# Cross-attentions of a decoder on one core: probabilities turned in 32x32 blocks by VectorE and carried by DMAs, the division moved behind the weighted sum

## The chip, the core and the metric

The kernel runs on one core of a Trainium2 chip. The metric is the device time of one execution in microseconds, as a median over runs. All data is fp32. The profile shows TensorE's matmuls (PE) and weight loads (PEld), VectorE (DVE), ScalarE (ACT), GpSimd (POOL), and the queues in which SP and ACT issue DMAs (SPq, ACTq).

## What is computed

Four decoder layers, each with self-attention, cross-attention and a mixture of experts, on x of 8 x 56 tokens of 256 features, each step with a residual and a layer norm. The cross-attentions of layers 0, 2 and 3 are latent attentions over a context of 1500 positions with 64 features. Cut to what matters:

```python
q_r = einsum('bshq,hqr->bhsr', q_big, W_qr)        # after two projections (and rope)
k_r = einsum('bld,hdr->bhlr', kv_r, W_kr)
scores = einsum('bhsr,bhlr->bhsl', q_r, k_r)       # 16 heads, s = 56, l = 1500
attn = softmax(scores, axis=-1)
ctx_c = einsum('bhsl,bld->bhsd', attn, kv_r)
ctx = einsum('bhsd,hkd->bhsk', ctx_c, w_kc_kv) ... @ Wo.T
```

## The kernel before

The twelve steps run one after the other, each as a stage in which every engine has its own program, written out in order; semaphores tie them together. `cross_attention` is the stage of layers 0, 2 and 3. Its first part folds the weights and makes the queries `q2` (16 heads of 56 tokens of 8 samples) and the matrices `cm`. Its second part, which the change is about, works through NU = 28 units. The 8 samples lie in J = 4 pairs, and a pair has UNITS = 7 units of 128 rows (head, token). A unit does the same 128 rows for both samples e = 0 and 1 of the pair, against 1500 positions of each, in LT = 12 blocks of LP = 125. With two samples there are 24 blocks of probabilities in a unit. The context of a sample is 64 features wide, so two matmuls on 64 rows or 64 columns of the array (halves r) go side by side. In the fourth unit of a pair (`SPLIT`) each half is divided between the two samples, so that it takes four matmuls where the others take two.

What a unit i goes through:

- PE, `score(i, k)` (L1035): for k = 0 to 2, 500 positions of each sample, into banks 0 to 2 (e = 0) and 3 to 5 (e = 1). These banks exist once: score(i, 0) waits for both exponentials of unit i - 1.
- DVE, `rowmax(i)`: three reductions of 500 (L1315), one of the three maxima (L1317), and one of 1500 for the other sample (L1320).
- ACT, `exp(i, e)` (L1236): 1500 elements from PSUM to `probs`, with the sum over the row by an accumulator read.
- DVE, `invert` (L1324) and `divide` (L1328): the reciprocal of the sum, and the division of 1500 probabilities, for each e.
- PE, `turn(i, k)` (L1122): 48 transposes (24 blocks of 125, by 64 rows each) into six banks; they leave PSUM in six copies of 512, two by DVE (L1334) and four by ACT (L1243), into `pT`.
- PE, `weigh(i)` (L1135): for each of 12 blocks and each half, `ctx_pos` times `pT`, summed in bank 6, 128 columns.
- DVE, `keep(i)` (L1341): the sum into `held`; POOL (L908) places it in `ctxT`. After the last unit DVE does both (`keep_last`, L1348).

PE's order is score(i), weigh(i - 2), turn(i - 1) for each i, and at the end project(0), weigh(26), project(1), turn(27), project(2), weigh(27), norms, project(3) (`project` is L1150). Each matmul counts as two instructions in the trace, a transpose as one. DVE's order in an iteration is rowmax(i), invert and divide (i, 0), keep(i - 2), its two copies of unit i - 1, invert and divide (i, 1). ACT's is exp(i, 0), exp(i, 1), its four copies of unit i - 1; in iteration 0 it also copies `cm` and the last queries (`cm_out(3)`, `place(7)`, L1195). SP issues the loads of the next stage's weights (`prefetch`, all through L125) once the last queries are placed, about when unit 0 is done.

## Time and profile before

| | us |
|---|---|
| median of 3 runs | 1667.23 |
| lowest, highest | 1664.79, 1677.47 |
| span of the profiled execution, first to last instruction | 1666.3 |
| PE busy (share of the span) | 1627.4 (98%) |
| DVE busy | 1113.9 (67%) |
| ACT busy | 749.9 (45%) |
| POOL busy | 239.1 (14%) |
| stretches of the 28 units of layers 0, 2, 3 (scores to the end of the stage) | 205 to 447, 829 to 1070, 1338 to 1582 |

The profile is of one execution, whose span is the time to which sums are compared; the median of the runs is 0.9 us above it. A group of instructions is named by its line in the kernel, the engine, the operation and the tiles written and read, with count, busy time and mean duration, and behind the last bar the idle time of the engine just before them and what ended it. Durations of neighbours on one engine overlap a little, so a period is read from starts. Matmul ends are modelled.

### The profile page before, as it was taken

Reading aid. Unit: us, or ns where it says so; the run is one execution under the profiler, and the core shown is the slowest. Engines: PE = TensorE matmul, PEld = TensorE weight load, DVE = VectorE, ACT = ScalarE, POOL = GpSimd, SP = SyncE. Lnnn points to the kernel's source line nnn. Section 1 sums busy time; section 2 is a strip of 40 time slices with the busy share of each in tenths; the row PEclk is TensorE's granted clock in tenths of the full one; section 3 lists DMA queues with packets and bytes.
Section 4 is the critical chain, followed back from the end, with each engine's and each line's share of the span. In section 5 each row is a group of like instructions: output and inputs, shape, how many; then the busy total and the mean of one; then the engine's idle time right before and its main releaser. Section 6 shows DMA issues by size and latency. Waiting matters only on the chain.

```text
span 1666.3 us, 35653 instructions
## 1 busy us (share of the span) xinstructions
PE 1627.4 (98%) x15234; PEld 1104.8 (66%) x15234; DVE 1113.9 (67%) x1974; ACT 749.9 (45%) x1297; POOL 239.1 (14%) x428
## 2 busy tenths in 40 slices
PE   9999999999999899999999999999999999999998
PEld 5575367777755666655377777764566767777765
DVE  3735899999566763266899999435445289999623
ACT  2223366666413641144366666312444366666411
POOL 0011300000010313011200000010455000000030
PEclk9999999999999999999999999999999999999999
DMA  8302020000040011051020000050300220000010
GB/s 280 86 13 83 1 78 2 2 2 2 2 187 1 2 59 40 1 133 48 1 97 2 2 2 2 4 240 0 64 1 1 114 89 2 2 2 2 2 44 11
DMA packets 35522, 71.10 MB, mean 43 GB/s; under 512 B 25359, under 2 KB 29775, under 8 KB 31433
## 3 DMA queue, kind: packets, MB, share of 16 engines
q1 hardware_dynamic: 35240, 68.71, 12.6%
q8 instruction: 121, 1.98, 0.5%
q14 instruction: 35, 0.29, 0.1%
q10 hardware_dynamic: 126, 0.11, 0.0%
HBM read 68.36 MB, written 0.46 MB: 41 GB/s over the span
## 4 chain that ended last, share of the span: by engine, by line
PE 89%; DVE 6%; ACT 2%; POOL 1%; issue 1%; DMA 1%; SPq 0%; DVEq 0%; POOLq 0%; ACTq 0%
PE ps L1122 14%; PE ps L1135 14%; PE ps L1035 13%; PE ps L1501 9%; PE ps L361 9%; PE ps L946 3%; PE ps L2599 3%; PE ps L1150 3%; PE ps L528 2%; PE ps L1961 2%; PE ps L956 1%; POOL arena L1795 1%; PE ps L2626 1%; PE ps L982 1%; PE ps L967 1%
## 5 line engine op out<-in xcount | busy, mean ns | idle before, releaser
L1236 ACT ACTIVATE arena<-ps,softmax_stats 128x1500 f32<-128x1500 f32 x168 | 253.8, 1511 | 193.0 <-DVE softmax_stats L1317 190.8
L1135 PEld LDWEIGHTS ps<-arena,ctx_pos 125*64 125x64 f32 x4608 | 222.3, 137 | 58.4 <-issue 55.4
L1122 PE MATMUL ps<-ident,arena 64*125 64x64 f32 x4032 | 239.1, 271 | 1.9 <-ACT arena L1236 1.6
L1135 PE MATMUL ps<-arena,ctx_pos 125*64 125x128 f32 (+1 forms) x4608 | 240.5, 262 | 0.0
L1122 PEld LDWEIGHTS ps<-ident,arena 64*125 64x125 f32 x4032 | 226.8, 185 | 17.0 <-issue 13.5
L1035 PE MATMUL ps<-ctx_feat,arena 64*128 64x500 f32 x1008 | 230.5, 590 | 0.0
L1243 ACT COPY arena<-ps 125x512 f32<-125x512 f32 x336 | 172.5, 600 | 77.9 <-PE ps L1122 77.9
L1315 DVE TENSOR_REDUCE softmax_stats<-ps 128x1 f32<-128x500 f32 x252 | 170.6, 678 | 49.0 <-PE ps L1035 48.6
L361 PE MATMUL ps<-arena 128*128 128x256 f32 x736 | 174.7, 383 | 3.5 <-DVE arena L1630 1.2
L1328 DVE TENSOR_SCALAR arena<-arena,softmax_stats 128x1500 f32<-128x1500 f32 x168 | 168.3, 1002 | 5.9
L1501 PE MATMUL ps<-x_feat,arena 128*128 128x448 f32 (+1 forms) x416 | 167.9, 549 | 1.2 <-DVE arena L1613 1.2
L361 PEld LDWEIGHTS ps<-arena 128*128 128x128 f32 x736 | 137.0, 190 | 40.9 <-issue 16.6
L908 POOL COPY arena<-arena 64x128 f32<-64x128 f32 (+1 forms) x186 | 51.1, 275 | 682.6 <-DVE arena L1341 676.5
L1320 DVE TENSOR_REDUCE softmax_stats<-ps 128x1 f32<-128x1500 f32 x84 | 143.6, 1709 | 0.0
L1035 PEld LDWEIGHTS ps<-ctx_feat,arena 64*128 64x128 f32 x1008 | 89.2, 187 | 80.0 <-issue 77.1
L1501 PEld LDWEIGHTS ps<-x_feat,arena 128*128 128x128 f32 (+1 forms) x416 | 79.3, 193 | 65.7 <-issue 61.7
L1334 DVE COPY arena<-ps 125x512 f32<-125x512 f32 x168 | 107.6, 682 | 12.8 <-PE ps L1122 12.5
L1577 ACT ACTIVATE arena<-ps 128x448 f32<-128x448 f32 (+1 forms) x52 | 28.2, 543 | 187.0 <-PE ps L1501 187.0
L1613 DVE TENSOR_TENSOR arena<-ps,arena 128x448 f32<-128x448 f32 x41 | 25.6, 624 | 115.6 <-ACT arena L1577 87.9
L946 PE MATMUL ps<-x_feat,arena 128*128 128x448 f32 x128 | 56.1, 563 | 0.2
L2599 PE MATMUL ps<-x_feat,arena 128*128 128x448 f32 x128 | 52.4, 552 | 1.2 <-issue 0.7
L2727 DVE TENSOR_TENSOR arena<-ps,arena 128x448 f32<-128x448 f32 x32 | 20.0, 625 | 46.0 <-ACT arena L2671 45.9
(324 smaller groups left out, 1931.7 us busy)
## 6 DMA issues: line engine op xcount, KB each, us to landing
ctx_pos<-in_ctx SPq DMA_DIRECT2D x1, 2688.0 KB
arena<-in_L1f_gate SPq DMA_DIRECT2D x1, 2304.0 KB, 12.1
arena<-in_L1f_up SPq DMA_DIRECT2D x1, 2304.0 KB, 17.0
arena<-in_L1f_down SPq DMA_DIRECT2D x1, 2304.0 KB, 7.8
arena<-in_L0a_Wq SPq DMA_DIRECT2D x1, 2048.0 KB, 10.9
arena<-in_L0a_Wc SPq DMA_DIRECT2D x1, 2048.0 KB, 18.8
arena<-in_L0x_Wq SPq DMA_DIRECT2D x1, 2048.0 KB, 9.9
arena<-in_L0x_Wo SPq DMA_DIRECT2D x1, 2048.0 KB, 8.3
```

The costliest lines, as they stand in the source:

```text
L361: m = c.nc.tensor.matmul(y_of(c, s, j), lhsT, rhs, start=False, stop=last, skip_group_check=True)
L946: m = nc.tensor.matmul(c.ps[:, 2 + h % 2, 0:NT], wq[:, k, h, :], c.x_feat[:, k, :, 0:T], start=(k == 0), stop=(k == KT - 1))
L1035: m = nc.tensor.matmul(sc[e][:, k, :], q[e * 64:(e + 1) * 64], c.ctx_feat[e * 64:(e + 1) * 64, j, k * 4 * LP:(k + 1) * 4 * LP], start=True ...
L1122: m = nc.tensor.transpose(c.ps[0:LP, turn_bank(i, k, r), n * 64:(n + 1) * 64], probs[i % 2][e][rows, l * LP:(l + 1) * LP], c.ident[rows, r ...
L1135: m = nc.tensor.matmul(y[r * 64:(r + 1) * 64, lo:hi], c.ctx_pos[:, j, l, e, :], pT[i % 2][:, lo // 64:hi // 64, LT * e + l, :], start=(l = ...
L1236: nc.scalar.activation(probs[i % 2][e].rearrange("p (k l) -> p k l", k=3), sc[e], ACT.Exp, bias=low[:, i % 4, e:e + 1], accum_out=total[:, ...
L1243: nc.scalar.copy(pT[i % 2][:, r, 8 * k:8 * k + 8, :], c.ps[0:LP, turn_bank(i, k, r), :].rearrange("p (s q) -> p s q", s=8)).then_inc(*a_in ...
L1315: nc.vector.tensor_reduce(peak[:, i % 4, k:k + 1], sc[0][:, k, :], AX.X, ALU.max).then_inc(*maxed.next())
L1320: nc.vector.tensor_reduce(low[:, i % 4, 1:2], sc[1], AX.XY, ALU.max, negate=True).then_inc(*lowered[1].next())
L1328: nc.vector.tensor_scalar(probs[i % 2][e], probs[i % 2][e], inv[:, i % 4, e:e + 1], None, ALU.mult).then_inc(*normed[e].next())
L1334: nc.vector.tensor_copy(pT[i % 2][:, r, 0:8, :], c.ps[0:LP, turn_bank(i, 0, r), :].rearrange("p (s q) -> p s q", s=8)).then_inc(*d_in.next())
L1501: m = nc.tensor.matmul(c.ps[0:m_, bank(n) + i, 0:NT], w[:, k, n * 128:n * 128 + m_], c.x_feat[:, k, :, 0:T], start=(k == 0), stop=(k == KT ...
```

## The change

It touches `cross_attention` alone. The exponential writes each block of 125 probabilities with a pitch of LQ = 128. Of the 24 blocks, the first BY_PE = 6 of sample 1 are still turned by PE: 12 transposes in place of 48, into the rest of bank 6 and into bank 7, and they leave PSUM in two copies of 384 by ACT. The other 18 are turned by two VectorE transposes (`turn_blocks`), of 12 x 128 = 1536 and 6 x 128 = 768 elements a partition. Each works in squares of 32x32: position 4q + g of a block goes, for g = 0 to 3, to partition q of a group of 32 in `blocks`, so the transposes read `probs` with a step of four elements. Every square is then on the partitions of its 32 rows, and SP moves it with four DMAs a unit: DMA `frm` reads 32 partitions (rows 32 frm and on), 4 x 576 elements of each, and writes 128 partitions, 576 elements (2304 bytes) of each, into `moved_to`: 288 KB a DMA, 1152 KB a unit. `weigh` takes its moving operand from `moved_to` or from `pT`.

The probabilities are no longer divided. DVE makes both reciprocals of a unit in one instruction after the transposes. POOL multiplies the identity by them (`diag`, two products of 128x128), PE multiplies ones by `diag` (`spread`, two matmuls, four in a split unit), which gives each column its reciprocal on all rows, ACT copies that to `rinv`, and POOL multiplies the held context by it where it copied before. Keeping the sum of `weigh` moves from DVE to ACT. In ACT's order the copies of unit i - 2 and the keeping of unit i - 3 stand ahead of exp(i, 0). The prefetch of the next stage is issued by ACT in iteration 0, as SP's queue holds the moves. Both `blocks` and `moved_to` have two buffers: the transposes of unit i wait until the moves of unit i - 2 have landed, and its moves until weigh(i - 2) is done. PE's order is score(i), weigh(i - 2), turn(i - 1), spread(i - 1).

```diff
-        "C": 23616, "Z": 25664, "buf": 27712, "rope": 3584, "PT": 0, "P": 6144, "RB": 12288}
...
+        "C": 23616, "Z": 25664, "buf": 27712, "rope": 3584, "PT": 0, "P": 6144, "TT": (12288, 25664), "RB": 14592}
...
+LQ, BY_PE = 32 * 4, 6
+RUN = 32 * (2 * LT - BY_PE)
...
-    pT = [c.at(o["PT"] + i * LT * 256, LT * 256, LP).rearrange("p (r s q) -> p r s q", r=2, q=64) for i in range(2)]
-    probs = [[c.at(o["P"] + (2 * i + e) * L, L) for e in range(2)] for i in range(2)]
-    held = [c.at(o["RB"] + 128 * i, 128) for i in range(2)]
...
+    blocks = [c.at(o["TT"][i], 4 * RUN).rearrange("p (g n) -> p g n", g=4) for i in range(2)]
+    moved_to = [c.at(o["PT"] + i * 4 * RUN, 4 * RUN).rearrange("p (g n) -> p g n", g=4) for i in range(2)]
+    pT = [c.at(o["PT"] + 8 * RUN + i * 128 * BY_PE, 128 * BY_PE, LP).rearrange("p (r l q) -> p r l q", r=2, q=64) for i in range(2)]
+    probs = [[c.at(o["P"] + (2 * i + e) * LT * LQ, LT * LQ) for e in range(2)] for i in range(2)]
+    held, rinv = ([c.at(o["RB"] + 256 * n + 128 * i, 128) for i in range(2)] for n in range(2))
+    diag = [c.at(o["RB"] + 512 + 256 * i, 256).rearrange("p (e n) -> p e n", e=2) for i in range(2)]
+    ones = c.at(o["RB"] + 1024, 64)
     low, total, inv = (c.sb_small[:, 8 * n:8 * n + 8].rearrange("p (i e) -> p i e", e=2) for n in range(3))
...
+    def turn_place(r):
+
+        return c.ps[0:LP, 7, 0:64 * BY_PE] if r else c.ps[0:LP, 6, 128:128 + 64 * BY_PE]
+
+    spread_ps = c.ps[:, 7, 64 * BY_PE:64 * BY_PE + 128]
...
-        sp.wait_ge(lat_in.handle, lat_in.at(4 * NH // 2))
-        prefetch(sp)
+        for i in range(NU):
+            sp.wait_ge(blocked[1].handle, blocked[1].at(i + 1))
+            if i >= 2:
+                sp.wait_ge(pv_mm.handle, pv_mm.at(i - 1))
+            for frm in range(4):
+                sp.dma_start(moved_to[i % 2][:, frm, :],
+                             blocks[i % 2][32 * frm:32 * frm + 32, :, :]).then_inc(moved[i % 2].handle, 16)
+                moved[i % 2].n += 16
...
-        for i in range(NU - 1):
+
+        def spread_out(i):
+            pool.wait_ge(recip.handle, recip.at(i + 1))
+            if i >= 4:
+                pool.wait_ge(ct_in.handle, ct_in.last())
+            if i >= 2:
+                pool.wait_ge(spread_mm.handle, spread_mm.at(i - 1))
+            for e in range(2):
+                nc.gpsimd.tensor_scalar(diag[i % 2][:, e, :], c.ident[:], inv[:, i % 4, e:e + 1], 1.0, ALU.mult, ALU.mult).then_inc(*diag_in.next())
+
+        def place_context(i):
             j, u = i // UNITS, i % UNITS
+            pool.wait_ge(diag_in.handle, diag_in.last())
+            pool.wait_ge(rinv_in.handle, rinv_in.at(i + 1))
             pool.wait_ge(kept.handle, kept.at(i + 1))
             for r, e, lo, hi in parts(u):
                 rows, at = slice(r * 64, (r + 1) * 64), 128 * u - HALF * (r ^ e)
-                nc.gpsimd.tensor_copy(ctxT[rows, 2 * j + e, at + lo:at + hi], held[i % 2][rows, lo:hi]).then_inc(*ct_in.next())
+                nc.gpsimd.tensor_tensor(ctxT[rows, 2 * j + e, at + lo:at + hi], held[i % 2][rows, lo:hi],
+                                        rinv[i % 2][rows, lo:hi], ALU.mult).then_inc(*ct_in.next())
+
+        for i in range(NU):
+            spread_out(i)
+            if i >= 3:
+                place_context(i - 3)
+        place_context(NU - 3)
+        place_context(NU - 2)
         pool.wait_ge(ct_in.handle, ct_in.last())
...
-            if i > 1 and k < 2:
-                pe.wait_ge(d_in.handle, d_in.at(2 * (i - 2) + 1 + k))
-            if i > 1 and k == 2:
-                pe.wait_ge(a_in.handle, a_in.at(4 * (i - 2) + 3))
...
-        def turn(i, k):
-
-            if k == turn_order(i)[0]:
-                for e in range(2):
-                    pe.wait_ge(normed[e].handle, normed[e].at(i + 1))
-            if k == 0 and i < NU - 1:
-                pe.wait_ge(exped[0].handle, exped[0].at(i + 2))
-            if k == 2 and i > 0:
-                pe.wait_ge(kept.handle, kept.at(i))
-            if i == 0 and k == 2:
+        def turn(i):
+
+            pe.wait_ge(exped[1].handle, exped[1].at(i + 1))
+            if i == 0:
                 pe.wait_ge(lat_in.handle, lat_in.at(4 * NH // 2))
                 pe.wait_ge(cm_act.handle, cm_act.at(3))
-            if k == (1 if i == 0 else 2) and i < NU - 1:
-                pe.wait_ge(exped[1].handle, exped[1].at(i + 2))
-            for n in range(8):
-                e, l = divmod(8 * k + n, LT)
+            else:
+                pe.wait_ge(b_in.handle, b_in.at(2 * i))
+                pe.wait_ge(rinv_in.handle, rinv_in.at(i))
+            for l in range(BY_PE):
                 for r in range(2):
                     rows = slice(r * 64, (r + 1) * 64)
-                    m = nc.tensor.transpose(c.ps[0:LP, turn_bank(i, k, r), n * 64:(n + 1) * 64],
-                                            probs[i % 2][e][rows, l * LP:(l + 1) * LP], c.ident[rows, rows])
-                    if n == 7:
+                    m = nc.tensor.transpose(turn_place(r)[:, l * 64:(l + 1) * 64],
+                                            probs[i % 2][1][rows, l * LQ:l * LQ + LP], c.ident[rows, rows])
+                    if l == BY_PE - 1:
                         m.then_inc(*(turned_hi if r else turned_lo).next())
 
+        def spread(i):
+
+            pe.wait_ge(diag_in.handle, diag_in.at(2 * i + 2))
+            for r, e, lo, hi in parts(i % UNITS):
+                m = nc.tensor.matmul(spread_ps[r * 64:(r + 1) * 64, lo:hi], ones, diag[i % 2][:, e, lo:hi], start=True, stop=True,
+                                     skip_group_check=True)
+            m.then_inc(*spread_mm.next())
+
         def weigh(i):
 
             j, u = i // UNITS, i % UNITS
-            pe.wait_ge(a_in.handle, a_in.at(4 * (i + 1)))
-            pe.wait_ge(d_in.handle, d_in.at(2 * (i + 1)))
+            pe.wait_ge(b_in.handle, b_in.at(2 * (i + 1)))
+            pe.wait_ge(moved[i % 2].handle, moved[i % 2].at(64 * (i // 2 + 1)))
+            if i > 0:
+                pe.wait_ge(kept.handle, kept.at(i))
             y = c.ps[:, 6, :]
             for l in range(LT):
                 for r, e, lo, hi in parts(u):
-                    m = nc.tensor.matmul(y[r * 64:(r + 1) * 64, lo:hi], c.ctx_pos[:, j, l, e, :],
-                                         pT[i % 2][:, lo // 64:hi // 64, LT * e + l, :], start=(l == 0 and lo == 0),
+                    if e == 1 and l < BY_PE:
+                        p = pT[i % 2][:, lo // 64:hi // 64, l, :]
+                    else:
+                        at = 32 * (LT * e + l - BY_PE * e)
+                        p = moved_to[i % 2][0:LP, lo // 32:hi // 32, at:at + 32]
+                    m = nc.tensor.matmul(y[r * 64:(r + 1) * 64, lo:hi], c.ctx_pos[:, j, l, e, :], p, start=(l == 0 and lo == 0),
                                          stop=(l == LT - 1), skip_group_check=True)
             m.then_inc(*pv_mm.next())
...
-            for k in turn_order(i - 1):
-                turn(i - 1, k)
-        pe.wait_ge(d_in.handle, d_in.at(2 * (NU - 1)))
+            turn(i - 1)
+            spread(i - 1)
         project(0)
         weigh(NU - 2)
         project(1)
-        for k in range(3):
-            turn(NU - 1, k)
+        turn(NU - 1)
+        spread(NU - 1)
...
-            nc.scalar.activation(probs[i % 2][e].rearrange("p (k l) -> p k l", k=3), sc[e],
-                                 ACT.Exp, bias=low[:, i % 4, e:e + 1],
+            nc.scalar.activation(probs[i % 2][e].rearrange("p (k l q) -> p k l q", k=3, l=4)[:, :, :, 0:LP],
+                                 sc[e].rearrange("p k (l q) -> p k l q", l=4), ACT.Exp, bias=low[:, i % 4, e:e + 1],
                                  accum_out=total[:, i % 4, e:e + 1]).then_inc(*exped[e].next())
 
-        def copy_turned(i, k, r):
-            done = turned_hi if r else turned_lo
-            act.wait_ge(done.handle, done.at(3 * i + turn_order(i).index(k) + 1))
-            nc.scalar.copy(pT[i % 2][:, r, 8 * k:8 * k + 8, :],
-                           c.ps[0:LP, turn_bank(i, k, r), :].rearrange("p (s q) -> p s q", s=8)).then_inc(*a_in.next())
-
-        for i in range(NU + 1):
+        def copy_turned(i, r):
+            if r:
+                act.wait_ge(turned_hi.handle, turned_hi.at(i + 1))
+                act.wait_ge(spread_mm.handle, spread_mm.at(i + 1))
+            else:
+                act.wait_ge(turned_lo.handle, turned_lo.at(i + 1))
+            nc.scalar.copy(pT[i % 2][:, r, :, :], turn_place(r).rearrange("p (l q) -> p l q", q=64)).then_inc(*b_in.next())
+
+        def keep(i):
+            act.wait_ge(pv_mm.handle, pv_mm.at(i + 1))
+            act.wait_ge(turned_lo.handle, turned_lo.at(i + 2))
+            if i >= 2:
+                act.wait_ge(ct_in.handle, ct_in.at(placed(i - 2)))
+            nc.scalar.copy(held[i % 2], c.ps[:, 6, 0:128]).then_inc(*kept.next())
+
+        def keep_spread(i):
+            act.wait_ge(spread_mm.handle, spread_mm.at(i + 1))
+            if i >= 2:
+                act.wait_ge(ct_in.handle, ct_in.at(placed(i - 2)))
+            nc.scalar.copy(rinv[i % 2], spread_ps).then_inc(*rinv_in.next())
+
+        for i in range(NU + 2):
+            if i >= 3:
+                keep(i - 3)
+            if i >= 2:
+                copy_turned(i - 2, 0)
+                copy_turned(i - 2, 1)
+                keep_spread(i - 2)
             if i < NU:
                 exp(i, 0)
                 exp(i, 1)
             if i == 0:
                 cm_out(3)
                 place(7)
-            if i >= 1:
-                copy_turned(i - 1, 1, 0)
-                copy_turned(i - 1, 1, 1)
-                copy_turned(i - 1, 2, 1)
-                copy_turned(i - 1, 2, 0)
+                act.wait_ge(lat_in.handle, lat_in.at(4 * NH // 2))
+                prefetch(act)
...
-        def invert(i, e):
+        def turn_blocks(i, e):
             dve.wait_ge(exped[e].handle, exped[e].at(i + 1))
-            nc.vector.reciprocal(inv[:, i % 4, e:e + 1], total[:, i % 4, e:e + 1]).then_inc(*recip[e].next())
-
-        def divide(i, e):
-            dve.wait_ge(recip[e].handle, recip[e].at(i + 1))
-            nc.vector.tensor_scalar(probs[i % 2][e], probs[i % 2][e], inv[:, i % 4, e:e + 1], None,
-                                    ALU.mult).then_inc(*normed[e].next())
-
-        def copy_turned(i, r):
-            done = turned_hi if r else turned_lo
-            dve.wait_ge(done.handle, done.at(3 * i + 1 + (i == 0)))
-            nc.vector.tensor_copy(pT[i % 2][:, r, 0:8, :],
-                                  c.ps[0:LP, turn_bank(i, 0, r), :].rearrange("p (s q) -> p s q", s=8)).then_inc(*d_in.next())
-
-        def keep(i):
-            dve.wait_ge(pv_mm.handle, pv_mm.at(i + 1))
-            if i >= 2:
-                dve.wait_ge(ct_in.handle, ct_in.at(placed(i - 2)))
-            nc.vector.tensor_copy(held[i % 2], c.ps[:, 6, 0:128]).then_inc(*kept.next())
+            if i == 0:
+                dve.wait_ge(cm_mm.handle, cm_mm.at(4))
+            if i >= 2 and e == 0:
+                dve.wait_ge(moved[i % 2].handle, moved[i % 2].at(64 * (i // 2)))
+            n = BY_PE * e
+            nc.vector.transpose(blocks[i % 2][:, :, 32 * LT * e:32 * (LT + (LT - n) * e)].rearrange("p g (l h) -> p g l h", h=32),
+                                probs[i % 2][e][:, n * LQ:].rearrange("p (l q g) -> p g l q", g=4, q=32)).then_inc(*blocked[e].next())
+
+        def invert(i):
+            nc.vector.reciprocal(inv[:, i % 4, :], total[:, i % 4, :]).then_inc(*recip.next())
 
         def keep_last(i):
             j, u = i // UNITS, i % UNITS
             dve.wait_ge(pv_mm.handle, pv_mm.at(i + 1))
+            dve.wait_ge(rinv_in.handle, rinv_in.at(i + 1))
             for r, e, lo, hi in parts(u):
                 rows, at = slice(r * 64, (r + 1) * 64), 128 * u - HALF * (r ^ e)
-                nc.vector.tensor_copy(ctxT[rows, 2 * j + e, at + lo:at + hi],
-                                      c.ps[rows, 6, lo:hi]).then_inc(*ct_last.next())
-
-        def normalise(i, e):
-            invert(i, e)
-            divide(i, e)
-
-        for i in range(NU + 1):
-            if i < NU:
-                rowmax(i)
-                if i == 0:
-                    cm_out(2)
-                normalise(i, 0)
-            if i >= 2:
-                keep(i - 2)
-            if i >= 1:
-                copy_turned(i - 1, 0)
-                copy_turned(i - 1, 1)
-            if i < NU:
-                normalise(i, 1)
+                nc.vector.tensor_tensor(ctxT[rows, 2 * j + e, at + lo:at + hi], c.ps[rows, 6, lo:hi], rinv[i % 2][rows, lo:hi],
+                                        ALU.mult).then_inc(*ct_last.next())
+
+        for i in range(NU):
+            rowmax(i)
+            if i == 0:
+                cm_out(2)
+            turn_blocks(i, 0)
+            turn_blocks(i, 1)
+            invert(i)
```

## Rows read from the trace of the kernel before

**Rows 1.** The page, shares of the chain that ended last by line.
```profile
PE ps L1122 14%; PE ps L1135 14%; PE ps L1035 13%; PE ps L1501 9%; PE ps L361 9%; PE ps L946 3%; PE ps L2599 3%; PE ps L1150 3%; PE ps L528 2%; PE ps L1961 2%; PE ps L956 1%; POOL arena L1795 1%; PE ps L2626 1%; PE ps L982 1%; PE ps L967 1%
```

**Rows 2.** Window over layer 0's units: length, busy us (instructions), PEclk, DMA share, GB/s.
```profile
205.00:447.00 242.00, 240.58 (x3284) 183.06 (x3284) 212.70 (x343) 151.24 (x232) 18.48 (x64) 1.00 0.04 15
```

**Rows 3.** The chain that ended last, layer 0: start us, us, what.
```profile
223.28 2.77 PE ps L1135 x48
...
315.54 2.76 PE ps L1122 x48
318.30 2.57 PE ps L1035 x12
320.87 2.77 PE ps L1135 x48
...
426.57 2.77 PE ps L1135 x48
```

**Rows 4.** Timeline of unit 27 of layer 0: start us, us, engine, instruction [idle before].
```profile
423.84 2.73 PE L1035 MATMUL ps<-ctx_feat,arena 64*128 64x500 f32 x12
...
424.93 0.68 DVE L1315 TENSOR_REDUCE softmax_stats<-ps 128x1 f32<-128x500 f32 x1 [0.24 <-PE ps L1035]
...
427.32 0.16 DVE L1317 TENSOR_REDUCE softmax_stats<-softmax_stats 128x1 f32<-128x3 f32 x1
...
427.51 1.51 ACT L1236 ACTIVATE arena<-ps,softmax_stats 128x1500 f32<-128x1500 f32 x1 [2.30 <-DVE softmax_stats L1317]
...
429.15 0.16 DVE L1324 RECIPROCAL softmax_stats<-softmax_stats 128x1 f32<-128x1 f32 x1
...
430.55 0.19 ACT L1236 ACTIVATION_READ_ACCUMULATOR arena<-ps,softmax_stats 128x1 f32 x1
```

**Rows 5.** Timelines of PE, DVE and ACT, layer 0's first units.
```profile
219.43 1.08 PE L1122 MATMUL ps<-ident,arena 64*125 64x64 f32 x16 [0.54 <-ACT arena L1236]
220.35 2.92 PE L1035 MATMUL ps<-ctx_feat,arena 64*128 64x500 f32 x12
...
206.86 1.83 DVE L1315 TENSOR_REDUCE softmax_stats<-ps 128x1 f32<-128x500 f32 x3
208.73 0.15 DVE L1317 TENSOR_REDUCE softmax_stats<-softmax_stats 128x1 f32<-128x3 f32 x1
...
213.03 1.43 ACT L1195 COPY arena<-ps 64x224 f32<-64x224 f32 x4
216.15 1.51 ACT L1236 ACTIVATE arena<-ps,softmax_stats 128x1500 f32<-128x1500 f32 x1 [1.69 <-DVE softmax_stats L1317]
...
219.19 0.19 ACT L1236 ACTIVATION_READ_ACCUMULATOR arena<-ps,softmax_stats 128x1 f32 x1
```

**Rows 6.** Groups by line and form, DVE, 768 and 1536 elements in SBUF.
```profile
L686 DVE TENSOR_TENSOR arena<-ctx_pos,arena 125x768 f32<-125x768 f32 x8 | 7.3, 950 | 0.0
L689 DVE TENSOR_TENSOR ctx_pos<-ctx_pos,arena 125x1536 f32<-125x1536 f32 x4 | 7.0, 1758 | 0.1
```

**Rows 7.** Groups, DVE, 28 elements: one operand of L2024 steps by seven.
```profile
L2024 DVE SCALAR_TENSOR_TENSOR arena<-arena 128x28 f32<-128x28 f32 x2 | 0.4, 209 | 0.1
...
L2008 DVE TENSOR_TENSOR arena<-arena 128x28 f32<-128x28 f32 x2 | 0.4, 188 | 0.1
```

**Rows 8.** Groups, POOL, two-input products of 448 and 224 elements.
```profile
L2539 POOL TENSOR_TENSOR arena<-arena 128x448 f32<-128x448 f32 x32 | 36.4, 1139 | 4.3
...
L1795 POOL TENSOR_TENSOR arena<-arena 128x224 f32<-128x224 f32 x10 | 6.8, 677 | 0.8
```

**Rows 9.** DMA issues with us to landing, SP's queue, and a window (columns as above).
```profile
arena<-in_L1a_W SPq DMA_DIRECT2D x1, 1024.0 KB, 4.9
...
727.75 18.44 SPq L125 DMA_DIRECT2D arena<-in_L2x_kcq  x32
...
216.49 0.55 SPq L125 DMA_DIRECT2D arena<-in_L0f_mix  x1
...
214.50:224.00 9.50, 8.87 (x82) 5.22 (x80) 8.55 (x13) 5.25 (x8) 0.00 (x0) 1.00 0.85 330
```

21 lines of the change are left out of this document (8 added, 13 removed).

## Prediction

> **What bounds the kernel now.** The page's chain that ended last comes first: three PE lines of the cross-attentions, turn (L1122), weigh (L1135) and score (L1035), hold 41% of it [rows 1]. A window over one such stage shows PE busy for 240.58 of 242.00 us, DVE for 212.70, ACT for 151.24, at a granted clock of 1.00 (2.4 GHz) [rows 2]. Inside the stage the chain is nothing but PE: weigh 2.77 us, turn 2.76, score 2.57, together 8.10 a unit; the weigh of unit 0 starts at 223.28 and that of unit 25 at 426.57, so with the split units in it a period is 203.29/25 = 8.13 us [rows 3]. The other two stages repeat this. A unit is therefore worth what it costs PE, until another engine or a chain of waits is longer than what is left.
>
> **PE.** Of 48 transposes 12 stay: 2.76 x 12/48 = 0.69 us. The spread adds two matmuls of the kind of weigh's 24: 2.77 x 2/24 = 0.23. The sum is 2.57 + 2.77 + 0.69 + 0.23 = 6.26 us. That is not the period, because the scores have one set of banks: score(i+1) waits for both exponentials of unit i.
>
> **The score loop**, from one timeline of a steady unit: score starts at 423.84, the reduction of the three maxima (L1317) at 427.32, 3.48 us later; the first exponential starts 0.19 after that, and the second one's accumulator read ends at 430.74, 3.23 later still [rows 4]. PE picks such a release up after 0.05 us (the read ends at 219.38, PE starts at 219.43) [rows 5]. The loop is 3.48 + 0.19 + 3.23 + 0.05 = 6.95 us. Today it lies under PE's 8.10; after the change it lies above PE's 6.26.
>
> **DVE's round.** The divisions and the copies out of PSUM go; two transposes of 1536 and 768 elements come. From L1317 until the first exponential has landed are 1.83 us (427.32 to 429.15) [rows 4]. No VectorE transpose is in the trace. Bound below: fp32 instructions between SBUF tiles with exactly 1536 and 768 elements took 1758 and 950 ns [rows 6]; neighbours overlap by about 0.1 (three reductions of 0.68 end after 1.83 us [rows 4, 5]), so 1.67 + 0.87. The reciprocal adds 0.07, the next three reductions 1.87 until L1317 (206.86 to 208.73) [rows 5]. The round is 1.83 + 1.67 + 0.87 + 0.07 + 1.87 = 6.31 us, 0.64 under the loop. That cover holds up to (2.54 + 0.64)/2304, about 1.35 ns an element; beyond it each 0.1 ns is 0.23 us a unit.
>
> It matters because the transposes read `probs` with a step of four elements. The nearest row with a step reads every seventh element: 28 of them took 209 ns where 28 dense ones took 188, 0.75 ns more an element [rows 7]. Bound above: GpSimd's fp32 slope, (1139 - 677)/224 = 2.06 ns an element [rows 8]. I take the lower end: count, type and memories of rows 6 are those of the transposes, the step is 16 bytes where that of rows 7 is 28, and 28 elements are few. The price with a step is rival B.
>
> The Trainium skill ("SBUF — State Buffer", Door 1: The DMA port swizzle) says that SBUF is read in 16-byte lines, that each wants two hits for full rate, and, a line further, that fp32 can be strode over by four for free. By its first half a transpose would pay as in rival B, by its second half nothing; no row here has a step of exactly 16 bytes.
>
> **ACT** keeps its exponentials and gets four copies, of 384, 384, 128 and 128 elements, for four of 512. They stand ahead of exp(i,0) and wait for PE's weigh, turn and spread of the iteration before, which end 6.26 - 0.75 - 2.57 = 2.9 us into a round; the second exponential ends at 3.4, the next starts 3.7 later. Hidden. **POOL** gets four small products, each below the 677 ns of a two-input one of 224 elements [rows 8]: under 2.7 us of 6.95, with 5 us between the reciprocal and the spread that needs them. Hidden.
>
> **The moves.** Four DMAs of 288 KB a unit, issued by SP. They may take from the end of the second transpose (4.4 us after L1317) to weigh(i), which follows score(i+2). Weigh starts 0.75 before L1317 [rows 3, 4], which makes 2 x 6.95 - 0.75 - 4.4 = 8.7 us, and PE's slack of 0.7 makes 9.4 free. From below: one load of 1024 KB landed in 4.9 us [rows 9]. From above: 32 small loads of 1.5 MB in all left SP in 18.44 us, 0.58 apart, 83 GB/s [rows 9]; four moves would take 14 us so. I take 5 to 7: their rows of 2304 bytes are nearer to the large loads, which ran at 330 GB/s [rows 9], and four issues cost SP 2.3. Hidden. If the cover goes, x us too many delay the score three units on, x/3 a unit; and with 1.18 MB a unit anything under 170 GB/s is itself the bound.
>
> The Trainium skill ("SBUF — State Buffer", the same section) gives 189 GB/s for 1 MiB on partitions 0 to 31, since they reach 8 of 16 ports; each move reads 32 partitions. By it a unit's moves take an estimated 6.2 us of the 6.95, still inside. No row here shows it.
>
> **The ends of a stage.** The prefetch moves from SP's queue to ACT's. ACT is done with its copies at 214.46 [rows 5]; five issues end at 217.04 on SP [rows 9], so the exponentials of unit 1 start at about 217.2 in place of 216.15. But score(2) then waits for them alone and not for a third of a turn: it starts near 220.5 where today it starts at 220.35 [rows 5]. 0.1 us lost. The first moves share the DMA engines with the prefetch (85% busy up to 224 [rows 9]); I put 1.5 us a stage on that, between 0 and 5. At the end turn(26) gives 2.76 - 0.69 - 0.23 less 0.6 of waiting for the last exponential, 1.2; turn(27) gives 1.84. The last moves have two projections and a weigh in front of them. 3.0 us gained.
>
> **The sum.** A stage: 25 x (8.13 - 6.95) = 29.5, + 3.0, - 1.6: 30.9 us. Three: 92.7. From the profiled span of 1666.3 that leaves 1573.6; the median of the runs lies 0.9 above the span: 1574.5 us.
>
> **The rivals.**
> A, the sum: 1574.5 us.
> B, the step costs the 0.75 ns of rows 7. The transposes take 2.54 + 2304 x 0.00075 = 4.27, DVE's round 8.04, and the bound has moved from PE to DVE. A stage: 25 x 0.09 + 3.0 - 2.9 (unit 1 is later by 1.3 more) = 2.4; about 1660 us. For it: the only row with a stepped read. Against it: its step is another.
> C, slower than before: a transpose costs GpSimd's 2.06 ns an element, 4.9 us with its fixed part; round 8.67, a stage loses 25 x 0.54 + 0.6. + 42 us: 1709. It decides from 1.84 ns an element on, where DVE's round is the old 8.13. For it: no row turns data, so a transpose may fill and drain one after the other. Against it: no streaming row of DVE is that slow.
> D, the moves land late: at 12 us in place of 9.4, 0.87 us a unit, + 65: 1640 us; even at 13.1 us. For it: no transfer from SBUF to SBUF is in the trace. Against it: that is more than twice the 4.9 us.
> PE's clock is no rival of weight: PE would be busy 6.26 of 6.95 us, 90%, and a stretch with 8.87 of 9.50 kept 1.00 [rows 9].
>
> **Chances.** A 0.52, B 0.20, C 0.12, D 0.10, anything else 0.06. A measurement of this kernel can't tell less than about 1% from no change, that is 1650.6 to 1683.9. Faster: A, most of D, a fourth of B and half of the rest, 0.67. Same: the rest of B, a little of C and D, 0.19. Slower: 0.14. The range goes from 1562 (moves and prefetch cost nothing, an end of 1.5 us more a stage saved) over D and B to 1668, and leaves out C and what is far. A's own range is 1562 to 1600.
>
> **What would show it.** Right: a unit of 6.9 to 7.1 us; transposes near 1.76 and 0.95 us; PE idle some 0.7 us a unit ahead of score, released by ACT's exponential; moves landing in under 9 us. B or C: 2.9 or 3.3 us for the 1536 elements, DVE without idle time in the stages, and no wait of PE on a DMA. D: PE idle ahead of weigh, released by a DMA. All of it would be wrong if ACT or POOL held PE at turn or at spread.

## The result, and the profile after

The change makes the kernel slower: 1697.95 us, the median of 4 runs (1688.27 to 1700.48), against 1670.59 for the kernel before on the same chip, a ratio of 1.0162 with a 95% interval of 1.0112 to 1.0211. Its profiled execution spans 1686.5 us where that of before spans 1666.3; it was the fastest of the four, so the traces show less loss (20 us) than the medians do (27 us).

The same window over layer 0's units, with the columns of [rows 2]:

```profile
205.00:460.00 255.00, 218.36 (x2486) 149.93 (x2486) 228.59 (x239) 123.49 (x233) 46.07 (x119) 0.95 0.63 144
```

TensorE has lost its work as planned (218 us busy of 255, where [rows 2] show 240.58 of 242), and VectorE has taken its place: 228.59 of 255. Its groups by line and form in a steady stretch (240 to 430 us) tell why:

```profile
L1381 DVE STREAM_TRANSPOSE arena<-arena 128x1536 f32<-128x1536 f32 x23 | 68.0, 2957 | 5.5 <-ACT arena L1270 5.3
...
L1381 DVE STREAM_TRANSPOSE arena<-arena 128x768 f32<-128x768 f32 x23 | 34.9, 1517 | 0.0
```

A turn of 1536 elements takes 2957 ns and not the 1758 of [rows 6], one of 768 takes 1517 and not 950. The slope is (2957 - 1517)/768 = 1.875 ns an element. What stands behind the second bar is VectorE's idle time before them: 5.5 us in 23 units, so VectorE's own work fills all but some 0.24 us of a unit. The period of a unit is told best by the start of the maximum's last step (L1317 before, L1369 after). All times in us:

| | first three periods, stages of layers 0, 2, 3 | mean of the last 21 |
|---|---|---|
| before | 7.2 8.1 8.1 / 7.2 8.1 8.1 / 7.3 8.1 8.1 | 8.13 / 8.13 / 8.13 |
| after | 10.1 9.7 8.1 / 10.1 9.0 11.3 / 10.2 9.6 11.6 | 8.38 / 8.41 / 8.39 |

From the first to the last unit of a stage the change costs 9.7, 13.1 and 13.3 us (228.33, 231.73 and 231.96 against 218.59, 218.58 and 218.67): 5.3 to 6.2 from the fourth period on, the rest in the first three. Behind the units it gains: from the last maximum to the next stage's first large matmul 33.5 us became 30.5 to 30.6.

A second thing stands in a steady unit, in the timeline of all engines (start us, us, engine, instruction, [idle before <- releaser]):

```profile
298.89 0.72 POOL L922 TENSOR_SCALAR arena<-ident,softmax_stats 128x128 f32<-128x128 f32 x2 [6.44 <-DVE softmax_stats L1385]
299.69 0.97 POOL L931 TENSOR_TENSOR arena<-arena 64x128 f32<-64x128 f32 x2
300.57 0.16 DVE L1369 TENSOR_REDUCE softmax_stats<-softmax_stats 128x1 f32<-128x3 f32 x1
...
300.76 0.27 ACT L1293 COPY arena<-ps 128x128 f32<-128x128 f32 x1 [4.04 <-POOL arena L931]
300.92 1.53 ACT L1270 ACTIVATE arena<-ps,softmax_stats 128x1500 f32<-128x1500 f32 x1
...
302.56 4.36 DVE L1381 STREAM_TRANSPOSE arena<-arena 128x1536 f32<-128x1536 f32 x2 [0.20 <-ACT arena L1270]
...
304.17 4.48 PE L1062 MATMUL ps<-ctx_feat,arena 64*128 64x500 f32 x12 [1.48 <-ACT arena L1270]
```

The exponential starts 0.35 us after the maximum, not the 0.19 of [rows 4]: ahead of it in ACT's order stands the copy of the spread reciprocals (keep_spread, L1293), and this waits for POOL's place_context (L931) of two units before, which in POOL's order stands behind spread_out (L922) of the newest unit, which waits for VectorE's reciprocal. So POOL lies in the loop: it stretches the period from VectorE's 8.06 to some 8.2. And the score at 304.17 takes 4.48 us, not 2.79. By windows of one unit each, columns as in [rows 2], the clock granted to TensorE had fallen:

```profile
330.60:338.80 8.20, 6.72 (x78) 4.75 (x76) 7.95 (x9) 4.18 (x8) 1.62 (x4) 0.99 0.62 130
338.80:347.00 8.20, 7.85 (x76) 5.00 (x74) 7.59 (x9) 3.86 (x7) 1.62 (x4) 0.80 0.68 148
```

0.80 is the mean of stretches at 2.4 and at 1.2 GHz; ahead of this score, and ahead of the one at 337.99 that the second window shows, TensorE had idled 1.48 us. The profiled execution has the highest mean clock of the four (0.975, the others 0.96 to 0.967), so the slower ones may hold more of such falls; only one is traced.

### The profile page after: what moved, and what is told of

Its sections match the earlier page's. It is cut to its first block and busy times, and to the rows that moved or that the text cites. A ratio compares the mean times of both kernels' runs of the same rounds, so it can differ in the third digit from the quotient of the medians.

```text
span 1686.5 us, 30955 instructions
## 1 busy us (share of the span) xinstructions
PE 1537.7 (91%) x12594; PEld 988.7 (59%) x12594; DVE 1161.5 (69%) x1641; ACT 664.9 (39%) x1294; POOL 326.2 (19%) x599
## 5 line engine op out<-in xcount | busy, mean ns | idle before, releaser
L1381 DVE STREAM_TRANSPOSE arena<-arena 128x1536 f32<-128x1536 f32 (+1 forms) x168 | 369.6, 2240 | 22.6 <-ACT arena L1270 16.4
L1062 PE MATMUL ps<-ctx_feat,arena 64*128 64x500 f32 x1008 | 267.6, 667 | 89.5 <-ACT arena L1270 89.4
L1062 PEld LDWEIGHTS ps<-ctx_feat,arena 64*128 64x128 f32 x1008 | 114.0, 207 | 188.3 <-issue 187.1
L922 POOL TENSOR_SCALAR arena<-ident,softmax_stats 128x128 f32<-128x128 f32 x168 | 60.4, 372 | 560.5 <-DVE softmax_stats L1385 560.5
L1293 ACT COPY arena<-ps 128x128 f32<-128x128 f32 x84 | 22.6, 268 | 306.9 <-POOL arena L931 306.9
L931 POOL TENSOR_TENSOR arena<-arena 64x128 f32<-64x128 f32 (+1 forms) x186 | 77.4, 417 | 28.5 <-ACT arena L1287 14.3
L1280 ACT COPY arena<-ps 125x384 f32<-125x384 f32 x168 | 73.9, 505 | 0.0
L1143 PE MATMUL ps<-ident,arena 64*125 64x64 f32 x1008 | 72.8, 277 | 0.9 <-ACT arena L1293 0.9
L1143 PEld LDWEIGHTS ps<-ident,arena 64*125 64x125 f32 x1008 | 61.5, 185 | 15.5 <-issue 14.7
L977 PE MATMUL ps<-x_feat,arena 128*128 128x448 f32 x128 | 56.1, 563 | 0.2
L910 POOL TENSOR_TENSOR arena<-arena 128x448 f32<-128x448 f32 x32 | 35.6, 1134 | 93.9 <-DVE arena L1340 93.9
```

Source lines behind the costliest of these rows:

```text
L922: nc.gpsimd.tensor_scalar(diag[i % 2][:, e, :], c.ident[:], inv[:, i % 4, e:e + 1], 1.0, ALU.mult, ALU.mult).then_inc(*diag_in.next())
L931: nc.gpsimd.tensor_tensor(ctxT[rows, 2 * j + e, at + lo:at + hi], held[i % 2][rows, lo:hi], rinv[i % 2][rows, lo:hi], ALU.mult).then_inc(* ...
L1062: m = nc.tensor.matmul(sc[e][:, k, :], q[e * 64:(e + 1) * 64], c.ctx_feat[e * 64:(e + 1) * 64, j, k * 4 * LP:(k + 1) * 4 * LP], start=True ...
L1143: m = nc.tensor.transpose(turn_place(r)[:, l * 64:(l + 1) * 64], probs[i % 2][1][rows, l * LQ:l * LQ + LP], c.ident[rows, rows])
L1280: nc.scalar.copy(pT[i % 2][:, r, :, :], turn_place(r).rearrange("p (l q) -> p l q", q=64)).then_inc(*b_in.next())
L1381: nc.vector.transpose(blocks[i % 2][:, :, 32 * LT * e:32 * (LT + (LT - n) * e)].rearrange("p g (l h) -> p g l h", h=32), probs[i % 2][e][: ...
```

## The experiments

**1. The price of the step by itself.** Behind the last stage of the kernel before, instructions of 128x1536 from SBUF to SBUF, with element step k of the read (`put` is dense):

```
+ nc.vector.tensor_copy(put, src(k))           # k = 1, 2, 3, 4, 5, 8, then a dense read and writes with step 4
+ nc.vector.transpose(sq(put), sq(src(k)))     # k = 1, 2, 3, 4, 8, then a dense read and writes with step 4
+ nc.scalar.copy(put, src(k)), nc.gpsimd.tensor_copy(put, src(k))    # k = 1, 4
```

> The kernel before with DVE, ACT and POOL instructions of 128x1536 behind its last stage (they compute nothing of the reference), once with the elements side by side and once with steps of 2, 3, 4, 5 and 8 elements. Theory S (the step of the read sets the price): tensor_copy and transpose both take about 1.6 us with no step and about 2.9 us with a step of 4, and lie near each other at every step. Theory T (turning in blocks costs 1.9 ns an element whatever it reads): the copies stay near 1.6 us, all transposes take about 2.9 us. If the price depends on the size of the step, steps of 2 and 3 lie below those of 4, 5 and 8.

The timeline of its end; the lines L2878 to L2890 are these 13 VectorE instructions in that order, L2896 and L2898 ACT's, L2904 and L2906 POOL's:

```profile
1689.47 0.96 DVE L2878 COPY arena<-arena 128x1536 f32<-128x1536 f32 x1
1690.47 0.96 DVE L2879 COPY arena<-arena 128x1536 f32<-128x1536 f32 x1
1691.46 1.19 DVE L2880 COPY arena<-arena 128x1536 f32<-128x1536 f32 x1
1692.69 1.52 DVE L2881 COPY arena<-arena 128x1536 f32<-128x1536 f32 x1
...
1695.81 1.54 DVE L2883 COPY arena<-arena 128x1536 f32<-128x1536 f32 x1
1697.38 1.53 DVE L2884 COPY arena<-arena 128x1536 f32<-128x1536 f32 x1
1698.95 1.78 DVE L2885 STREAM_TRANSPOSE arena<-arena 128x1536 f32<-128x1536 f32 x1
1700.76 1.78 DVE L2886 STREAM_TRANSPOSE arena<-arena 128x1536 f32<-128x1536 f32 x1
1702.57 2.21 DVE L2887 STREAM_TRANSPOSE arena<-arena 128x1536 f32<-128x1536 f32 x1
1704.81 2.88 DVE L2888 STREAM_TRANSPOSE arena<-arena 128x1536 f32<-128x1536 f32 x1
1707.72 2.92 DVE L2889 STREAM_TRANSPOSE arena<-arena 128x1536 f32<-128x1536 f32 x1
1710.68 2.88 DVE L2890 STREAM_TRANSPOSE arena<-arena 128x1536 f32<-128x1536 f32 x1
...
1737.77 1.47 ACT L2896 COPY arena<-arena 128x1536 f32<-128x1536 f32 x1 [70.44 <-DVE arena L2890]
1739.28 2.89 ACT L2898 COPY arena<-arena 128x1536 f32<-128x1536 f32 x1
...
1746.65 1.47 POOL L2904 COPY arena<-arena 128x1536 f32<-128x1536 f32 x1 [127.38 <-ACT arena L2898]
1748.18 2.88 POOL L2906 COPY arena<-arena 128x1536 f32<-128x1536 f32 x1
```

A transpose costs 1.78 us dense and with a step of two, 2.21 with three, 2.88 with four and 2.92 with eight, and a dense read written with a step of four costs the same 2.88. Theory T falls: it is the step that makes a transpose dear, and its size matters up to four. Theory S holds in that, but not in the prices of the copies, which it put near the transposes' at every step: a copy takes 0.96 us dense and 1.52 with four. The ratio is alike (1.58 and 1.62); the price of the step is not, 0.36 ns an element for a copy and 0.72 for a transpose.

**2. The same kernel with dense blocks.** Left out: the order of the positions, so the context is a wrong mixture.

```
- probs[i % 2][e][:, n * LQ:].rearrange("p (l q g) -> p g l q", g=4, q=32)
+ probs[i % 2][e][:, n * LQ:].rearrange("p (l g q) -> p g l q", g=4, q=32)
```

> After, with the blocks read side by side (positions of a block land in another order than the weights' context rows, so the context is a wrong mixture). Theory S: the transposes fall from 2.96 and 1.52 us to about 1.76 and 0.95, DVE's round from 8.06 to about 6.3, and the period to what comes next, 6.95 (the score loop) to 7.4 us; 75 periods at 1.0 to 1.4 us less than 8.34: 1575 to 1625 us. Theory T: the transposes keep 2.96 us and the time stays at 1698, within 5.

1608.38 us, 0.9639 of before (0.9597 to 0.9681), 90 us under the change; steady periods of 7.07 to 7.09. Its groups from 240 to 400 us:

```profile
L1381 DVE STREAM_TRANSPOSE arena<-arena 128x1536 f32<-128x1536 f32 x23 | 40.9, 1779 | 1.1
...
L1381 DVE STREAM_TRANSPOSE arena<-arena 128x768 f32<-128x768 f32 x23 | 21.5, 935 | 0.0
```

The transposes cost 1779 + 935 in place of 2957 + 1517 ns, and nothing else was changed: the step is the main cause. But the third period lost more than in the change: periods of 8.3, 8.8 and 13.5 us in layer 0, with a weigh that waits for a move, in TensorE's timeline:

```profile
226.92 5.39 PE L1171 MATMUL ps<-arena,ctx_pos 125*64 125x128 f32 x48 [3.91 <-DMA arena<-arena]
```

**3. POOL out of the loop.** The change with four buffers for the spread reciprocals in place of two:

```
  def keep_spread(i):
-     if i >= 2: act.wait_ge(ct_in.handle, ct_in.at(placed(i - 2)))
-     nc.scalar.copy(rinv[i % 2], spread_ps)
+     if i >= 4: act.wait_ge(ct_in.handle, ct_in.at(placed(i - 4)))
+     nc.scalar.copy(rinv[i % 4], spread_ps)
```

> After, with four buffers for the spread reciprocals, so that ACT's keep_spread no longer waits for POOL's place_context of two units earlier. If POOL's chain (reciprocal, spread_out, place_context, ACT copy, exp) sets the units of 8.23 us, these fall to 8.06 and the time by up to 15 x 0.17 a stage, 8 us in all: 1690. If DVE's round sets them anyway: no change, 1698 within 2.

1683.7 us, 1.0093 of before (1.0062 to 1.0123): 14 us under the change by the medians, more than expected, and 11.7 us less in the units of the three traced stages. The two intervals overlap a little, so the size is rough. The waits from 240 to 430 us (us in total, times, longest), first of the change, then of this kernel:

```profile
ACT arena L1293 <- POOL arena L931: 93.4, 23, 4.6
```

```profile
ACT arena L1271 <- DVE softmax_stats L1370: 91.4, 24, 4.4
```

The copy's wait for POOL is gone and the exponential waits for the maximum alone. Most steady units now take 8.04 to 8.10 us. Gone are the three long units a stage in which place_context has four pieces in place of two, the split ones (8.7 to 9.3 us in the change). Left are units of 8.76 us, at places that differ from stage to stage, each behind a score of this kind (timeline of TensorE):

```profile
277.58 4.48 PE L1063 MATMUL ps<-ctx_feat,arena 64*128 64x500 f32 x12 [1.29 <-ACT arena L1271]
```

**4. The clock.** Such a score takes mostly 4.48 us in place of 2.79 and lengthens its unit by 0.7 with the four buffers, by 0.6 in the change. Behind the first three units there are 16 of them in the three stages of the change, 13 with the four buffers, none in the kernel before, each in the one execution that is traced. Two matmuls of 384 columns that nothing reads keep TensorE from idling:

```
          pe.wait_ge(rinv_in.handle, rinv_in.at(i))
+         keep_busy(c, 7, 2, None, 64 * BY_PE)
```

> After, with two matmuls of 384 columns that nothing reads ahead of each turn (1.3 us more of PE a unit, in its idle time). If the granted clock falls in the units where PE idles, and the score matmuls at 4.48 us then make the units of 8.7 to 9.3 us: the clock stays at 1.00, these units go back to 8.06 to 8.23, 0.2 us a period less on the mean, 5 us a stage, 1680 to 1690. If the slow units have another cause: 1698 or, with PE's work in the way, up to 1710.

In the change: 1707.55 us, 1.0239 of before (1.0206 to 1.0271), 10 us slower than the change by the medians, where 8 to 18 faster was expected. No steady score was slow and the granted clock of the window (205 to 460 us) rose from 0.95 to 0.99, but now nearly every unit took the 8.23 to 8.3 us of the POOL loop, the split ones about 8.75. In the change a unit that a slow score had lengthened let the next one run at 8.06 to 8.1. By the traces the last 21 periods of the stages gained 3.1 us in all and the first three lost 5.6.

> After with four buffers for the spread reciprocals and two matmuls of 384 columns that nothing reads ahead of each turn. With POOL out of the loop the fillers cannot lengthen it (7.5 us of PE's work in 8.06). If the fallen clock costs the 13 steady units with a score of 4.48 us their 0.7 us each: no such score, all steady periods 8.04 to 8.12, 9 us less than with the four buffers alone, 1675 us. If these units are long for another reason: they stay, at 1684.

With the four buffers: 1693.03 us, 1.0144 (1.0089 to 1.02), 9 us slower by the medians than without fillers where 9 faster was expected; the intervals overlap. Again no slow score, but most periods are 8.14 to 8.18 and not 8.06, and the turns of 1536 elements take 3013 ns in place of 2973 (its groups by form, 240 to 430 us):

```profile
L1383 DVE STREAM_TRANSPOSE arena<-arena 128x1536 f32<-128x1536 f32 x24 | 72.3, 3013 | 1.2
```

In the traces the last 21 periods gained 1.4 us in all by these fillers, where 9 was expected, and the first three lost 4.8. So the falls of the clock are real and cost 16 x 0.7 = 11 us at most in the traced execution of the change, but fillers give nearly all of it back. Why a turn is longer beside a filler stays open.

**5. Where the first units lose.** Two forms of one edit. The loads for the next stage (`prefetch`, on ACT's queue behind unit 0) are kept in a list and issued later: (a) whole, one a unit from the fourth on, in the change; (b) in pieces of 320 columns (160 KB), one a unit from the third on, in the change.

```
-             prefetch(act)
+             prefetch(later)               # collects (to, from, semaphore)
+         if i >= 3 and later.q:            # (b): i >= 2, pieces of 320 columns
+             to, frm, inc = later.q.pop(0)
+             act.dma_start(to, frm).then_inc(*inc)
```

> After with one thing changed: the loads for the next stage issued one a unit from the fourth unit on. If they hold up the first moves (third period of 11.3 and 11.6 us in the second and third of the stages, 9.7 in the second period of the first): 2 to 5 us less a stage, 1683 to 1692 us. If the start is long only because of DVE's dearer round (10.1 us in the first period): 1698 within 3 us.

(a): 1701.17 us, 1.0197 of before (1.0162 to 1.0232): no gain, where 1683 to 1692 was expected. The third periods fell to 8.07, but one of 8.6 to 13.8 us came where the loads were issued.

> After with one thing changed: the next stage's loads in the same pieces of 160 KB, one a unit from the third unit on. If the whole loads cost the change its periods of 9.6 and 11.4 us: 3 to 5 us less a stage, 1683 to 1689 us. If not: 1698 within 3 us.

(b): 1690.47 us, 1.0125 of before (1.0081 to 1.0169): 7.5 us under the change by the medians, just short of the 9 to 15 expected. The intervals overlap, so the time alone does not show a gain; the traces do, with third periods of 8.1 in all stages (8.1, 11.3 and 11.6 in the change) and 5.0 us less in the units of the three stages. The first moves tell why. Those of unit 0 in layer 2 (the view of the line that issues them), of the change:

```profile
DMA to landing us min/median/max: 9.1/10.6/11.2
```

and with the loads in pieces:

```profile
DMA to landing us min/median/max: 4.1/5.2/5.4
```

**6. Both mendings, with the step kept** (3 and 5b together).

> After with the four reciprocal buffers and the loads in pieces together, and the blocks still read with the step of four. If DVE's round of 8.06 us is what is left against the kernel before: 1697.95 - 14 - 7.5 = 1676 us, still 5 to 12 us above before, and 84 above the same kernel with the blocks read side by side (1592.6), that is 75 periods x 0.99 and some 10 us at the starts. If the two mendings overlap: nearer 1683.

1667.78 us, 1.0003 of before (0.9985 to 1.0021): 30 us under the change, not 21.5. The last 21 periods have a mean of 8.07 in all three stages, where 3 alone has 8.14, 8.27 and 8.20: the trace of this kernel has only two slow scores behind the first three units (the fifth unit in layers 0 and 3, periods of 8.76), where 3 has 13, and 11 times 0.7 us is near the 8.7 us that came on top. It is no lucky profile: the mean clock is 0.983 to 0.989 in the ten executions of this kernel, 0.967 to 0.98 in the eight of 3. Why the clock held here, with TensorE as idle as in 3, the traces don't tell; it stays open, and the two ran on different chips.

> The kernel with four buffers and loads in pieces, and the same fillers. Its steady units had no score at a lower clock. If the clock is all that fillers can mend: 1668 within 3 us. If its profile was a lucky one and other runs have such units: up to 9 us less, 1659.

1683.35 us, 1.0075 (1.0049 to 1.0101): with fillers 16 us slower, neither of the two times expected. The last 21 periods have means of 8.19 to 8.27, with single ones up to 9.07. There was next to nothing left to mend, and the fillers' own cost shows alone.

What remains in the kernel with both mendings is VectorE's round, and at 8.07 it is worth nearly what TensorE's 8.13 was; what the shorter end of a stage and the 0.06 us a period gain, the first units lose. So there is no difference to before.

**7. The dense read with the right result.** The columns of `ctx_feat` are put into the blocks' order once, in the first stage, by a matmul with a permuted identity where a transpose stood (positions of the six blocks that TensorE turns stay as they were); each turn then reads runs of 32 side by side. With the four buffers of 3:

```
-   m = nc.tensor.transpose(to, c.ctx_pos[:, j, k, :, :], c.ident[0:LP, 0:LP])
+   m = nc.tensor.matmul(to, c.ctx_pos[:, j, k, :, :], c.perm[:, :], start=True, stop=True)     # k >= BY_PE
...
-   probs[i % 2][e][:, n * LQ:].rearrange("p (l q g) -> p g l q", g=4, q=32)
+   bass.AP(frm.tensor, frm.offset + 93, [list(frm.ap[0]), [-31, 4], [LQ, LT - n], [1, 32]])
```

> The change with blocks read side by side and the columns of the context features put in the blocks' order once, where they are made in the first stage (a matmul with a permuted identity in place of the transpose), and four buffers for the spread reciprocals. If only the step of the read made the transposes dear: 1.76 us and 0.95 us, periods of 7.07 us as in the run without the step, and 1600 to 1612 us; the permuted columns cost the first stage 0 to 5 us. If a run of 32 elements that does not begin on a multiple of 16 bytes costs more: transposes above 2.0 us and 1625 us or more.

1610.25 us, 0.9652 of before (0.9617 to 0.9687), inside the expected 1600 to 1612. The transposes take 1778 and 935 ns: runs of 32 elements that begin on no multiple of 16 bytes cost nothing. The first stage pays for the permuted columns: unit 0's maximum stands at 212.1 us where it stood at 206.6 without them.

**8. What sets the period of 7.07.** Three runs on the kernel of 7.

> The kernel with the permuted columns and four reciprocal buffers, with the moves of the first two units of a stage alone; all later units weigh with the blocks of those two, so the context is wrong. If the loop from score to exp sets the period: it stays at 7.07 us and only what the moves delayed near the start goes (third periods of 12.3 to 15.2 us), 5 to 8 us a stage, 1586 to 1597 us. If the moves' traffic also slows the steady part: periods below 7.0 us.

This one moves only the first two units' blocks and computes a wrong context with them: 1608.18 us, 0.9647 of before (0.9622 to 0.9672), 11 us over the expected range. The steady period stays at 7.07, so the moves are hidden there. The third periods did not go (11.0, 14.3, 16.4 us): the moves that the loads hold up are just those of the first two units, which this kernel kept.

The next two keep all moves. "The kernel just described" is the kernel of 7 in the first expectation, and in the second it is that of the first.

> The kernel just described, and the loads for the next stage issued one a unit from the fourth unit on, instead of all behind the first. If these loads hold up the first moves (third period 13.5 to 14.5 us in the dense run, against 7.07): the first three periods fall from 30.6 to about 25 us a stage, 5 us less each, 1585 to 1595 us. If the start is long for another cause: the same time as the kernel just described, within 3 us.

1607.52 us, 0.9633 (0.9591 to 0.9676), and not the 1585 to 1595 expected: as in 5a the long period only wandered, to 12.1, 10.5 and 15.2 us.

> The kernel just described with 4 blocks turned by TensorE instead of 6, and 20 by VectorE. With 6, PE has 2.79 + 2.84 + 0.87 + 0.44 = 6.94 us of work a unit in a period of 7.07; with 4 it has 0.29 less, DVE 256 elements at 1.05 ns = 0.27 more (6.6). If PE's work sets the period: it falls to 6.95 at most, where the loop score, maximum, exp, score (3.48 + 0.19 + 3.23 + 0.05) binds: 9 us less in all. If the moves, 11% larger, bind: PE waits for DMA and the time rises.

1612.48 us, 0.9666 (0.9631 to 0.9701), most periods still 7.07, though TensorE has 0.29 us less to do: its work does not set them. The loop does, in the rows of one unit of this kernel:

```profile
301.77 0.16 DVE L1401 TENSOR_REDUCE softmax_stats<-softmax_stats 128x1 f32<-128x3 f32 x1
...
301.96 1.52 ACT L1298 ACTIVATE arena<-ps,softmax_stats 128x1500 f32<-128x1500 f32 x1 [2.97 <-DVE softmax_stats L1401]
...
305.01 0.19 ACT L1298 ACTIVATION_READ_ACCUMULATOR arena<-ps,softmax_stats 128x1 f32 x1
...
305.34 2.79 PE L1090 MATMUL ps<-ctx_feat,arena 64*128 64x500 f32 x12 [0.26 <-ACT arena L1298]
...
308.84 0.16 DVE L1401 TENSOR_REDUCE softmax_stats<-softmax_stats 128x1 f32<-128x3 f32 x1
```

**9. The dense read, four buffers and loads in pieces together.**

> The kernel with the permuted columns and four reciprocal buffers, the next stage's loads cut into pieces of 160 KB and issued one a unit from the third unit on. Whole loads of 1280 to 1792 KB, issued early or late, each time lengthened one period (12.1, 10.5 and 15.2 us in place of 7.07 when they were issued from the fourth unit). If it is their share of the DMA engines that holds up the moves: no period but the first two is over 7.3, 5.0, 3.5 and 8.1 us less, about 1591 us. If the pieces disturb the moves as much in sum: small delays in many periods and the time stays near 1607.

1592.59 us, 0.9555 of before (0.9506 to 0.9604): 73 us under the kernel before measured beside it (1665.47) and 105 under the change. From the third period on nearly all are 7.07, four of 7.5 to 8.1. Each of these four stands two units behind one whose four moves took 9.5 to 10.2 us from the end of its transposes to the last landing, where all others took 9.2 or less: here the moves are only just hidden. With the step kept and all else alike (6) it was 1667.78; the step alone is 75 us.

## Why the prediction was wrong, step by step

**PE.** Right in kind: PE is not what sets the period. In size, the turn's 0.69 and the spread's 0.23 us measured 0.87 and 0.44 (L1143 and L1152), so that PE's sum is 6.94 and not 6.26. That costs nothing, as the run with four blocks shows.

**The score loop.** Right as a bound, seen only once the step was gone: 3.50 + 0.19 + 3.24 + 0.14 = 7.07 us in the rows above, predicted 6.95. The pick-up by PE was the term too small, 0.14 in place of 0.05. The 0.12 us in all make 9 us in 75 periods.

**DVE's round: the step that failed.** "I take the lower end." The working had put beside it that each 0.1 ns over 1.35 is 0.23 us a unit ((2.54 + 0.64)/2304 is 1.38), and the only row with a stepped read said +0.75 ns [rows 7]. It was set aside because 28 bytes are not 16 and 28 elements are few. The step of 16 bytes cost (2957 - 1517)/768 less (1779 - 935)/768, 1.875 - 1.10 = 0.78 ns an element, so rival B was the right one: transposes of 4.36 us from start to end (predicted 4.27) and a round of 8.06 (8.04). That its price came out nearly to the digit is luck. The 0.75 is 21 ns over 28 elements between two different operations, and by the calibration the price of a step depends on the operation: 0.36 ns for a copy, 0.72 for a transpose. The lower end was chosen by the likeness of count and memories, and the one thing in which the rows differed was the thing in dispute. The right use of [rows 6] was for the dense part alone: 1779 and 935 ns measured against 1758 and 950, and 1.78 us in the calibration. There too the operation matters, since a dense copy of the same size takes 0.96; no row of before told which of the two a transpose is like.

The Trainium skill ("SBUF — State Buffer", Door 1: The DMA port swizzle) had both halves of the answer: two hits on a 16-byte line for full rate, and four fp32 to stride over for free. The runs side with the first half: steps of two are free, three cost a part, four the full price.

**ACT and POOL "Hidden".** Wrong. The sizes were right (POOL's 0.72 + 0.97 us are under the 2.7 allowed), but I asked whether each piece of work fits into a unit, and not what stands ahead of what: a copy with a wait for POOL stands ahead of the exponential in ACT's order, and POOL's product behind the newest unit's reciprocal. The sign that the prediction gave for this, PE held at turn or spread, did not show: held were ACT's copy and the exponential behind it. The edit that mends it gave 14 us.

**The moves.** Hidden, as predicted: leaving them out changed no steady period, and rival D is out. But the size was short. The 5 to 7 us were to cover all four moves of a unit, from the end of the second transpose to the last landing. One move landed in 5.2 us from its own issue, and the four issues lie 2.8 us from first to last, so a unit's moves took 8.0 us (median from the fourth unit on, longest 9.7) of the 9.4 allowed. The page's row of the DMA issues of the change (the last number is us to landing), and the issues of the unit whose transposes end at 298.74:

```profile
arena<-arena SPq DMA_DIRECT2D x336, 288.0 KB, 5.2
```

```profile
L894 SPq DMA_DIRECT2D arena<-arena x4: 543/1055/1867, 298.8 to 301.6; - x4
...
DMA to landing us min/median/max: 4.3/5.1/5.4
```

**The ends of a stage.** The tail gained 2.9 us in layer 0 (3.0 predicted). The start lost more than the 1.6 of the sum: 4.5 to 7.9 us over the first three periods (rival B had 2.9 for this, with a later unit 1). The moves that meet the whole loads were in the sum with 1.5 us and cost more than 3 in the third periods of layers 2 and 3. Two things were missing. In the first round VectorE also has a copy of `cm` (0.69 us) and then waits 1.26 us for a matmul of the first part, so the first period is 2.9 us longer in every stage. And PE idles and comes back at a lower clock, which shows in the second period. Not all of that is the change's: the calibration run, whose code is that of before up to its end, has a score of 4.43 us at the same place and a second period of 9.6 where the profile of before has 8.1. In the change's timelines of VectorE and of TensorE, layer 0:

```profile
208.59 0.69 DVE L1322 COPY arena<-ps 128x512 f32<-128x512 f32 x1
210.53 4.39 DVE L1381 STREAM_TRANSPOSE arena<-arena 128x1536 f32<-128x1536 f32 x2 [1.26 <-PE ps L968]
...
220.32 5.37 PE L1062 MATMUL ps<-ctx_feat,arena 64*128 64x500 f32 x12 [3.93 <-ACT arena L1270]
226.54 2.84 PE L1171 MATMUL ps<-arena,ctx_pos 125*64 125x128 f32 x48 [0.86 <-DMA arena<-arena]
```

**The clock** "no rival of weight". The 90% was worked out for a period of 6.95 us; under one of 8.2 TensorE was busy for 85% (162.4 of 190 us, 240 to 430) and idled up to 1.8 us ahead of a score, and the clock did fall in 16 units. The stretch taken as proof [rows 9] was busier than that.

**The sum again.** With both mendings and the step kept, the kernel is rival B without its flaws: 1667.8 us, where B had 1660; its first six periods lose 4.4 us in layer 0 where B had 2.9 a stage, and its period is 8.07 and not 8.04. From there to the change it is 30 us more: POOL in the loop, the falls of the clock, and whole loads against the first moves, 14 and 7.5 us by the medians of the single edits, the rest in what they do together. How the 30 us divide exactly is not settled: between two executions of one code the stretches outside these stages differ by up to 6 us (403.40 and 289.91 us between the units of two stages in the kernel before, 401.01 and 295.90 in the calibration run, which is the same up to its end). In the traced executions of kernels with the change they range wider, from 397.9 to 405.8 and from 284.3 to 297.2.
